# Plain and expert feed-forward layers as one program of sixteen batches

## The reference

```python
x = stencil(x)                        # layer 0
x = attention_block(x)                # layer 1, first half
h = layernorm(x) * g2 + beta2         # layer 1, plain feed-forward
x = x + gelu2(h @ W1 + b1) @ W2 + b2  # W1 512 x 2048, W2 2048 x 512
e = itok_B_0_7                        # layer 2, one of 8 experts for each batch
o = gelu(x @ Wi[e] + bi[e]) @ Wo[e] + bo[e]
y = layernorm(o + x) * gamma[e] + beta[e]
U_o, V_o = gram_schmidt(U), gram_schmidt(V)     # layer 3, 512 x 32 each
strength = sigmoid(relu(mean(y) @ gw1.T + gb1) @ gw2.T + gb2) * sigmoid(safety)
out = y + strength * (y @ basis @ basis.T[:, :32] @ resp_w.T + resp_b + safety_bias)
```

## Time and profile before

| | us |
|---|---|
| median of three timed runs | 2818.02 (2813.56 to 2820.8) |
| the profiled execution, device time | 2812.16 |
| its span, first to last instruction | 2810.4 |
| TensorE busy in the span | 2645.2 (94%) |
| mean granted clock of TensorE | 0.98 of full speed |

### The profile page before, as it was taken

The page is one execution under the profiler, slowest core; times in us unless marked ns, Lnnn a source line. Parts: engine busy times, 40 slices in busy tenths (PEclk is TensorE's granted clock), DMA queues, the critical chain, the costliest instruction groups (busy, mean ns, idle before and its releaser), DMA issues. The chain is left out here.

```text
span 2810.4 us, 46285 instructions
## 1 busy us (share of the span) xinstructions
PE 2645.2 (94%) x17088; PEld 2035.8 (72%) x17088; DVE 1698.8 (60%) x3339; ACT 1025.5 (36%) x2160; POOL 1027.3 (37%) x765
## 2 busy tenths in 40 slices
PE   6984999999999999969999999999799999999997
PEld 2433777777777777657888888888677877877775
DVE  8975777777777777655444444443466564565543
ACT  1113666666666666611111111111122233223222
POOL 1004677776777767442101110110333222222210
PEclk9996999999999999989999999999899999999998
DMA  4324564555646555442011101100454344243311
GB/s 152 123 83 155 172 191 139 191 151 177 192 142 187 152 176 166 121 126 76 1 31 31 31 0 31 31 16 1 129 158 131 117 124 127 91 126 120 102 51 38
DMA packets 212633, 305.99 MB, mean 109 GB/s; under 512 B 14266, under 2 KB 93178, under 8 KB 209722
## 3 DMA queue, kind: packets, MB, share of 16 engines
q1 hardware_dynamic: 210682, 299.88, 34.2%
q0 software_dynamic: 1728, 3.16, 0.4%
HBM read 268.94 MB, written 34.05 MB: 108 GB/s over the span
## 5 line engine op out<-in xcount | busy, mean ns | idle before, releaser
L780 POOL TENSOR_TENSOR at_bias<-at_bias,at_mask 128x1024 f32<-128x1024 f32 x224 | 480.0, 2146 | 248.7 <-DMA at_bias<-in_fside_Bx16xSxS 247.0
L1145 DVE CUSTOM_DVE_ANT_0 at_bias<-at_bias,at_bank_score 128x512 f32<-128x512 f32 x512 | 338.1, 681 | 182.3 <-PE at_bank_score L1011 137.7
L872 ACT ACTIVATE at_y<-at_bias,at_nmax 128x512 f32<-128x512 f32 x512 | 366.4, 716 | 22.4 <-DVE at_nmax L1145 22.4
L1553 POOL TENSOR_SCALAR expert_WH<-expert_stage 128x1024 fp32r<-128x1024 f32 x128 | 159.2, 1244 | 455.2 <-DMA expert_stage<-in_L_cond_Wo 227.9
L1018 PE MATMUL at_bank_probT<-at_ident,at_y 128*128 128x128 f32 x2048 | 313.2, 280 | 6.6 <-ACT at_y L872 6.6
L1636 ACT ACTIVATE ff_g<-ff_bank_hid,ff_b1c 128x512 f32<-128x512 f32 x128 | 88.3, 690 | 610.0 <-PE ff_bank_hid L98 610.0
L1917 DVE CAST ff_gH<-ff_g 128x512 fp32r<-128x512 f32 x128 | 71.4, 557 | 388.0 <-ACT ff_g L1636 387.7
L1018 PEld LDWEIGHTS at_bank_probT<-at_ident,at_y 128*128 128x128 f32 x2048 | 228.2, 141 | 94.3 <-issue 65.6
L1919 DVE TENSOR_TENSOR expert_gL<-expert_g,expert_gH 128x512 fp32r<-128x512 f32 x128 | 95.4, 745 | 310.6 <-ACT expert_g L1636 310.5
L1635 ACT ACTIVATE expert_gH<-expert_bank_hid,expert_b1c 128x512 fp32r<-128x512 f32 x128 | 88.3, 690 | 530.3 <-PE expert_bank_hid L98 530.2
L880 ACT ACTIVATE at_probT<-at_bank_probT 128x512 f32<-128x512 f32 x256 | 153.2, 598 | 270.0 <-PE at_bank_probT L1018 158.3
(11 more groups left out here) (330 smaller groups left out, 5643.7 us busy)
## 6 DMA issues: line engine op xcount, KB each, us to landing
at_bias<-in_fside_Bx16xSxS SPq DMA_DIRECT2D x256, 512.0 KB, 3.8
expert_stage<-in_L_cond_Wi SPq DMA_DIRECT2D x128, 256.0 KB, 2.9
expert_stage<-in_L_cond_Wo SPq DMA_DIRECT2D x128, 256.0 KB, 3.0
st_f<-in_x SPq DMA_DIRECT2D x8, 1024.0 KB, 6.9
x_after_layer<-st_y SPq DMA_DIRECT2D x8, 1024.0 KB, 4.8
at_x<-x_after_layer SPq DMA_DIRECT2D x32, 256.0 KB, 5.0
x_after_attention<-at_x SPq DMA_DIRECT2D x32, 256.0 KB, 2.2
ff_x<-x_after_attention SPq DMA_DIRECT2D x32, 256.0 KB, 4.3
```

The lines of the kernel that those rows point to most:

```text
L780: pool.tensor_tensor(bias[i % NB][:, :, :], bias[i % NB][:, :, :], mask[:, i // 2 % R, :].unsqueeze(1).to_broadcast([P, 2, S]), ALU.add).t ...
L872: act.activation(prob[u % 2][:, :], bias[u // 2 % NB][:, u % 2, :], ACT.Exp, scale=-1.0, bias=nmax[:, u % 4:u % 4 + 1], accum_out=sums[:, ...
L1145: dve.tensor_tensor_reduce(t, t, pS[u % HC][:, :], -1.0, 3.0e38, ALU.add, ALU.min, nmax[:, u % 4:u % 4 + 1]).then_inc(s_max, 1)
L1553: pool.tensor_scalar(WH[:, f, :], stage[f % 2][:, :], 1.0, 0.0, ALU.mult, ALU.add).then_inc(s_wh, 1)
```

## The change

The two programs become one, `feed_forwards`, with BATCHES = 16: n = 0 to 7 are the plain batches, n = 8 to 15 the expert batches. There is one set of tiles and semaphores; the stores, the clearing and the barrier between the layers go, and a batch of x2 is read back from DRAM while later ones are still being made. Units are numbered through: 0 to 15 plain, 16 to 143 expert. The schedule functions are now

```diff
-        UNITS = B * FC
+        BATCHES = 2 * B
+        UNITS = FC + B * FC
+        LEAD = (B - 1) * FC
         def units_by(s):
-            return 1 if s < 0 else min(s + FC - 1, 3 + 3 * s // 2, UNITS)
+            return max(min(s + 2, FC), min(s - LEAD + FC - 1, UNITS))
+        def highs_by(s):
+            return max(min(s + 4, FC), min(s - LEAD + FC, UNITS))
+        def loads_by(s):
+            return FC if s < LEAD else min(units_by(s) + 2, UNITS)
```

so from step 112 (the start of plain batch 7) one unit is loaded, split high and split low per step, into the chunk that the batch is through with. SyncE's list, with row loads one batch ahead and the stores of batch 7 behind its sixteen unit loads:

```diff
+            for n in range(B):
+                if n > 0:
+                    load_x(n + 1)
+                if n == B - 1:
+                    sp.wait_ge(s_tr, B * C)
+                    sp.dma_start(xn[:, 2, 0:P], a["L2_cond_bi"].rearrange("e (f p) -> (e f) p", p=P)).then_inc(s_bi, 16)
+                    sp.wait_ge(s_idx, 16)
+                    load_bias(0)
+                    for f in range(FC):
+                        load_units(n * FC + f)
+                for r in range(R):
+                    sp.wait_ge(s_res, n * R + r + 1)
+                    store_row(n, r)
```

The constants go into xn (free after the transposes of batch 7) and not into x[1]; GpSimd issues them at the start of batch 7, ahead of that batch's norms and high halves:

```diff
+            def high(g):
+                f = g % FC
+                pool.wait_ge(s_stage[f % 2], 32 * (g // 2 + 1))
+                if g >= FC:
+                    pool.wait_ge(s_w2, LEAD + g - FC + 1)
+            for n in range(BATCHES):
+                if n == B - 1:
+                    expert_constants()
```

The hidden biases are turned in plain batch 7 (TensorE behind chunk 3, VectorE in chunk 4, into the bank tr and not the last bank out). VectorE's order in a step of batch 7 is gelu split, low half, Gram-Schmidt; at the end of every batch come `h_split(n + 1)` and `residual(n)`:

```diff
+                    gelu_split(n, f)
+                    if n > 0:
+                        for g in range(units_by(s - 1), units_by(s)):
+                            low(g)
+                    if n == B - 1 and f == 4:
+                        hidden_biases()
+                    if B - 1 <= n < BATCHES - 1 and f == 4:
+                        pick_bias(n + 1 - B)
+                    if n < B:
+                        gram_schmidt(n, f)
```

and TensorE's transposes of batch 8 stand between two output groups of batch 7:

```diff
             def transposes(n):
+                src = x[n % 2] if n >= B else xn
                 for m in range(C):
+                    if m == 0 and 0 < n <= B:
+                        pe.wait_ge(s_gcopy, n * GS)
+                    if m == 0 and n == B:
+                        pe.wait_ge(s_pre, 1)
...
+                if n + 1 < BATCHES:
+                    transposes(n + 1)
                 output(n, FC - 1)
```

More of the change, by code:

```diff
@@ new lines, in feed_forwards @@
+        warm = sb("warm", [P, 1])
+        rw = sb("rw", [KR, D], F32R)
+        feats = sb("feats", [KR, S], F32R)
+        hilo = sb("hilo", [P, 2])
+        small = sb("small", [RANK, 3, RANK])
+        with ExitStack() as plain_only:
+            early = Names(nc, plain_only, "ff")
+            h32 = [early.sb(f"h32_{s}", [P, S]) for s in range(2)]
+            xn = early.sb("xn", [P, R, D])
+            later = early.sb("later", [P, RANK, RANK])
+        gamma_b = sb("gamma_b", [P, D])
+        beta_b = sb("beta_b", [P, D])
@@ L1418, in expert_of, with load_row @@
[L1418 to L1429, removed]
+            def load_row(n, r):
+                wait(sp, s_st[n % 2][r], n // 2 * 16)
+                src = rows_at(x_in, n) if n < B else rows_at(x_mid, n - B)
+                sp.dma_start(x[n % 2][:, r, :], src[:, r, :]).then_inc(s_x[n % 2], 16)
@@ L1577, in _ @@
[L1577 to L1594 removed]
+            power(1)
@@ L1598, in body @@
                                            ALU.pow).then_inc(s_nrm, 1)
-                    if not expert and first and f + 3 < FC:
-                        high(0, f + 3)
-                    if f == 5 and not expert and first:
-                        bias(0, 0, 0)
-                    if f == 8 and not expert and not last:
-                        power(n + 1, n + 2)
-                        bias(n + 1, 1 - slot, j if slot == 0 else j + 1)
-            in_order(pool, body)
-            if expert:
-                power(B - 1, B)
+                    for g in range(highs_by(s - 1), highs_by(s)):
+                        high(g)
@@ L1904, in h_split @@
                         wait(dve, s_hid, n * FC)
-                    if not expert:
+                    if n < B:
                         dve.wait_ge(s_h32, n * C + m + 1)
@@ L2097, in body @@
+            ln_apply(0)
+            low(0)
+            h_split(0)
+            for n in range(BATCHES):
                 for f in range(FC):
-                    if first and not expert and f + 1 < FC:
-                        low(0, f + 1)
+                    s = n * FC + f
+                    if n == 0 and f + 1 < FC:
+                        low(f + 1)
                     gelu_split(n, f)
-                    if expert and not first and f >= 4:
-                        tail(n - 1, 1 - slot, f)
@@ L2103, in body @@
-                    if expert:
-                        s = n * FC + f
-                        for u in range(units_by(s - 1) + (s == 0), units_by(s)):
-                            low(u // FC, u % FC)
-                    if expert and not last and f == 4:
-                        pick_bias(n + 1, 1 - slot)
-                    if expert and not first and f < 4:
-                        tail(n - 1, 1 - slot, f)
-                    if expert and first:
+                    if n > B and f >= 4:
+                        tail(n - B - 1, f)
```

632 lines of the change are left out of this document (284 added, 348 removed).

## The result

| | before | changed |
|---|---|---|
| median of timed runs, us | 2815.79 (4 runs, 2812.98 to 2820.8) | 2798.61 (4 runs, 2797.12 to 2800.1) |
| profiled execution: device time, us | 2812.16 | 2799.17 |
| its span, us | 2810.4 | 2797.5 |

The ratio is 0.9938, with a 95% interval from 0.9924 to 0.9952: 17.2 us less, faster by more than 0.3%. The forecast was 2800.2, with 17.8 us less; the measured median is inside its range of 2794 to 2811.

What follows compares the result with a forecast made beforehand. TensorE, busy 94%, bounds the kernel. 23.07 - 5.4 - 0.3 - 0 - 0.2 - 0.5 + 1.17 = 17.8 us less, from the 2818.02 median to 2800.2; range 2794 to 2811.

Steps and rivals of the forecast that it cites:

- The removed pause: Between the last plain product and first expert output: 20.50 us idle, 2.20 slow clock and 0.37 wait, together 23.07, all removed.
- The transposes with their wait: Batch 8's transposes before plain batch 7's last output group, waiting for VectorE: 5.4 us cost, bounds 2.8 and 7.2.
- The clock: At the new boundary, slow products after the transposes' wait: 0.5 us cost, bounds 0 and 2.2.
- The first output of batch 8: Wait before the first expert output product may remain: 0.2 us cost, bounds 0 and 0.4.
- The table load: Gelu table load on ScalarE, 1.28 us, stays ahead of the first expert gelu, nothing on the path; at most 1.28 if uncovered.
- Batch 7: Added loads, high and low halves cost TensorE 0 (bounds 0 and 2.6); VectorE 51 of 93 us; hidden-bias transpose 0.3.
- the constants at nothing: Ten constant DMAs and memsets on GpSimd's queue at batch 7's start, 5.5 us, ahead of the first high half: cost 0.
- The hidden-bias transpose: This transpose and its copy move into plain batch 7: 0.3 us cost, bounds 0.1 and 0.5.
- The first rival: Stalls in batch 7: late Gram products, 1 us at each of eight places, gain 9.8, 2808 us; chance 0.07.
- the fourth: Slower: the weight pipeline starves, a low half waiting for a late load holds VectorE; 27 us lost, 2827; chance 0.04.
- The port: Rival: 15 high halves on GpSimd each delay TensorE by 1.06 us, 15.9 of the gain lost, 2816 us; chance 0.04.
- The first expert batches: One chunk per step split, not one and a half: wait at first expert batch's end 2.22 to 1.05, -1.17 us.

## Why the prediction was right, step by step

- The removed pause. 23.07 us were to go and 5.4 + 0.2 + 0.5 to come: 16.97; measured 16.07. The transposes with their wait take 1983.59 - 1978.18 = 5.41 us, forecast 5.4. That these meet so well is partly luck, as the next lines show.

Timeline of DVE there in the changed kernel:

```profile
1977.44 1.22 DVE L1856 TENSOR_TENSOR ff_WL<-ff_stage,ff_WH 128x1024 fp32r<-128x1024 f32 x1
1978.58 1.01 DVE L1947 TENSOR_SCALAR ff_nrm<-ff_nrm 128x2 f32<-128x2 f32 x1
...
1981.68 1.29 DVE L1895 TENSOR_TENSOR ff_hL<-ff_bank_tr,ff_hH 128x512 fp32r<-128x512 f32 x2
```

The order is the one forecast: low half, Gram-Schmidt step, split. GpSimd's instruction fell on the first small step (1.01 where it is 0.16 in the earlier trace rows) and not on the low half. It cost 0.85 us where the forecast had allowed 0.34, so the wait is 3.21 and not 2 to 3. Against that the 0.3 for the last four transposes was not needed (no wait stands before them), and the sum had counted the last transposes by their record of 1.32 us, although the next product starts 1.08 after them.
- The clock. This term was mis-sized: 0.5 forecast, 1.57 measured, within its bound of 2.2. It had been put between a wait of 2.22 us without a loss and one of 2.59 with 1.3; the wait came out at 3.21, above both. The length of the wait does not settle the loss, though (last section).
- The first output of batch 8: 0.2 forecast, none measured. The table load, on ACT's timeline at 1984.59, lies beside the last output group of batch 7, one group earlier than forecast, and ScalarE is idle for 4.95 us after it: it cost nothing, as forecast.

```profile
1984.59 1.28 ACT L1632 ACT_TABLE_LOAD   x1
```

- Batch 7. Here the sum was wrong: 0.3 forecast, bound 3.1, measured 3.76. VectorE's load was right (51 of 93). The failed step is the one that put the constants at nothing, together with two beside it: that the first high half comes three groups (8.2 us) into the batch, and that a unit's load takes its median of 2.9 us. The first high half came 23.2 us in, since its unit was issued at 17.2, behind stores, rows and the bias loads. The beginning of batch 7 is no average place, since 1 MB of stores, 1 MB of rows, the constants and two units meet there. The first unit took 1904.18 - 1898.12 = 6.1 us to its high half. The hidden-bias transpose itself was nothing there: without the stall the batch takes 93.49 us against 93.47. The first rival named the right symptom, a late Gram product, but in eight places instead of one, and its reason, GpSimd's instruction on top of VectorE's, is only part of this one (1.6 us of the backlog); the fourth had the mechanism, a low half that waits for a late load and holds VectorE, at a price of 3.8 and not of 27.
- The port. The two engines do hold each other up (a low half of 2.07 us for 1.22) and it cannot be found on TensorE once the units are early: with 15 high halves in batch 7, that batch takes 93.5 us with and without them. The Trainium skill's rule ("SBUF — State Buffer", Who interferes with whom), by which a VectorE instruction with two SBUF inputs and a GpSimd instruction that reads SBUF exclude each other, agrees with that low half, 2.07 us beside GpSimd's high half. As a price for the kernel it was nothing by itself; where VectorE is already late, as in the changed kernel's batch 7, it adds to the wait.
- The first expert batches. 1.17 forecast and measured at the boundary; 2.1 more inside the next batch, which I had not looked for, come with the slower catch-up, which the forecast had credited with the boundary alone. They are why the total comes near although batch 7 cost 3.5 us more than forecast and the boundary won 0.9 less: forecast 17.8, traces 15.4, timed 17.2. The mechanism held; that the median came within 2 us of the forecast is in part luck, a missed loss against a missed gain.
- A slip in the rows: the stretch 1411 to 1504 of the earlier trace rows, called batch 1, is plain batch 2 (its transposes start at 1411.12). Batch 1 has no more idle time (93.56 busy of 94), so nothing hangs on it.

## What to carry to other kernels

Where two stages become one pipeline, every chain that crosses the seam must start early: rows and weights each held about half of what the boundary gave. What moves ahead of a seam must be costed with the transfers that already start there, not with the median landing time, and an in-order engine that waits for one late load hands the wait to everything queued behind it. Order an engine's queue by who waits longest: the step that nobody needs until later (here the last Gram-Schmidt step) goes behind the one that TensorE stands for.

## What was not expected of the hardware

A TensorE wait can cost more than its length, and its length does not say whether. With the output group behind it (twelve products, 2.72 us at full speed) as the measure: a wait of 1.57 us brought 1.71 of loss (bias copy moved), 1.85 brought 1.70, 3.04 brought 2.18 (Gram-Schmidt step moved) and 3.21 brought 1.57, all at the 1.2 GHz level of the clock. Waits of 1.05 brought some 0.1, and so did the 2.22 us at the first expert boundary of the kernel before, longer than two of those with a loss. Stretches around that wait (kernel before) and behind the one of 3.04:

```profile
2088.00:2091.00 3.00, 1.93 (x12) 1.63 (x13) 2.22 (x4) 1.20 (x2) 1.05 (x1) 1.00 0.74 241
...
1918.00:1921.00 3.00, 3.00 (x8) 2.32 (x8) 0.00 (x0) 0.00 (x0) 0.00 (x0) 0.50 0.53 175
```

What decides between the two is not shown by these runs.

And ten DMAs of 0.34 MB together (one of 256 KB, one of 64, the others of at most 4), in a stretch with the DMA engines 0.88 busy, delayed the landing of four 256 KB stores: a median of 5.3 us from issue in the changed kernel, 3.1 with the constants later. That held the four row loads behind them on SyncE's queue: 5.93 us and not 3.37 (5.86 to 6.24 in the other kernels that have constants and rows together there).
